# First stage of a vision tower kernel: the attention products issued ahead of the rank matmuls in every group

## The reference

```
tokens = einsum('bpi,hi->bph', patches, W) + b        # 64 patches of 28x28x3 per image, 128 features
h = concat([cls, tokens]) * pos_embed
n = layernorm(h)                                      # attention over a strictly causal window
scores = <n_t, n_s>; alpha = softmax(scores); c_t = sum alpha n_s
h = h + sigmoid(concat([c_t, n_t]) @ W_c)
z = layernorm(layernorm(h)); gate = softmax((z @ router_w + router_b) / 0.7)
mix = the two best of 16 experts: silu(z @ ew1 + eb1) @ ew2 + eb2, weighted by gate
moe = mix + 0.25 * shared expert
out = h + layernorm(h) + moe + silu(layernorm(moe) @ ff_w1 + ff_b1) @ ff_w2 + ff_b2
```

## Time and profile before

| what | value |
|---|---|
| median of three runs | 907.61 us (907.56 to 908.23) |
| span of the profiled execution | 972.0 us |
| TensorE busy in the span | 896.2 us, 92% |
| VectorE, ScalarE, GpSimd busy | 676.2, 599.5, 438.8 us |
| mean granted TensorE clock | 0.975 of full |
| DMA | 192 GB/s over the span |

### The profile page before, as it was taken

The page is one execution under the profiler, slowest core; times in us unless marked ns, Lnnn a source line. Parts: engine busy times, 40 slices in busy tenths (PEclk is TensorE's granted clock), DMA queues, the critical chain, the costliest instruction groups (busy, mean ns, idle before and its releaser), DMA issues. The chain is left out here.

```text
span 972.0 us, 22164 instructions
## 1 busy us (share of the span) xinstructions
PE 896.2 (92%) x5920; PEld 801.2 (82%) x5920; DVE 676.2 (70%) x2244; ACT 599.5 (62%) x1064; POOL 438.8 (45%) x374
## 2 busy tenths in 40 slices
PE   2999999989999999999889999999999899789999
PEld 2788888778878888888779889898999899679888
DVE  8377877757877887787556666666676675488884
ACT  3567666656666666777645565555555565477766
POOL 6012554425555545554451445455555464334342
PEclk9999999979999999999879999999999999989999
DMA  9999999977788888767137687777778675334432
GB/s 225 224 221 225 242 247 240 237 205 210 213 228 218 214 216 219 194 216 213 50 105 215 196 227 218 214 219 228 216 224 236 184 221 166 107 82 115 107 103 57
DMA packets 194299, 186.96 MB, mean 192 GB/s; under 512 B 16797, under 2 KB 168698, under 8 KB 194010
## 3 DMA queue, kind: packets, MB, share of 16 engines
q1 hardware_dynamic: 183168, 166.24, 65.2%
q0 software_dynamic: 9376, 19.42, 6.1%
q10 hardware_dynamic: 1722, 0.93, 0.5%
HBM read 150.48 MB, written 36.04 MB: 192 GB/s over the span
## 5 line engine op out<-in xcount | busy, mean ns | idle before, releaser
L1435 PE MATMUL bank<-xf,wp 128*128 128x256 f32 x1280 | 314.0, 394 | 8.4 <-ACT xf L632 5.4
L1435 PEld LDWEIGHTS bank<-xf,wp 128*128 128x128 f32 x1280 | 237.7, 192 | 51.6 <-issue 7.4
L916 POOL DMA_INDIRECT y_tok<-region,dsti x160 | 162.9, 1018 | 164.9 <-DVE region L1268 119.0
L874 POOL TENSOR_TENSOR rstd<-var,neghalf 128x4 f32<-128x4 f32 (+2 forms) x51 | 80.6, 1580 | 287.9 <-DVE var L1030 156.4
L632 ACT ACTIVATE xf<-region 128x1024 f32<-128x1024 f32 x160 | 174.0, 1137 | 18.3 <-DVE region L947 18.3
L890 POOL DMA_INDIRECT z_rows<-z,posg x130 | 157.3, 1210 | 52.5 <-issue 52.2
L798 ACT ACTIVATE region<-bank,cols 128x256 f32<-128x256 f32 x320 | 132.3, 476 | 55.2 <-PE bank L1626 37.2
L1637 PE MATMUL bank<-region 128*128 128x128 f32 x1280 | 156.8, 275 | 1.1 <-DVE region L1268 1.0
L1637 PEld LDWEIGHTS bank<-region 128*128 128x128 f32 x1280 | 150.4, 192 | 1.7 <-issue 1.5
L1626 PE MATMUL bank<-parts 128*128 128x256 f32 x960 | 136.6, 290 | 14.2 <-DVE parts L1279 8.8
L1626 PEld LDWEIGHTS bank<-parts 128*128 128x128 f32 x960 | 119.6, 190 | 25.7 <-issue 19.0
(11 more groups left out here) (183 smaller groups left out, 1232.3 us busy)
## 6 DMA issues: line engine op xcount, KB each, us to landing
region<-in_x SPq DMA_DIRECT2D x384, 196.0 KB
region<-in_L_ffn_ew SPq DMA_DIRECT2D x160, 256.0 KB
region<-z_rows SPq DMA_DIRECT2D x80, 130.0 KB
region<-y_tok SPq DMA_DIRECT2D x16, 512.0 KB, 3.6
ht_dram<-hT SPq DMA_DIRECT2D x16, 256.0 KB
r_dram<-rr SPq DMA_DIRECT2D x16, 256.0 KB
region<-ht_dram SPq DMA_DIRECT2D x16, 256.0 KB, 5.5
region<-r_dram SPq DMA_DIRECT2D x16, 256.0 KB
```

What stands on the lines that cost most here:

```text
L874: pool.tensor_tensor(dst, var, neghalf[:, 0:var.shape[1]], ALU.pow).then_inc(ready, 1)
L916: pool.indirect_dma_start(y_tok, bass.IndirectOffsetOnAxis(dsti[n % 2][:, i:i + 1], 0), yout[n % 2][:, i], None).then_inc(y_free[n % 2], 16)
L1435: ins = pe.matmul(out_cols, wp[:, s], cols_in, start=s == 0, stop=s == MAIN - 1)
```

## The change

In TensorE's `body`, `attend(g)` is called directly behind `project(g)` in all groups, and `ranks(g, nt)` behind it. Before, it stood so in the last group only, and behind `ranks` in groups 0 to 14. No instruction is added or taken away, and no semaphore is changed.

```
                 patches(10, 12)
                 project(g)
+                attend(g)
                 if fill:
-                    attend(g)
                     sh_up(5)
                 ranks(g, nt)
-                if not fill:
-                    attend(g)
```

## The result

The changed kernel took 913.26 us (median of six runs, 910.37 to 915.05), the kernel before 907.62 us in as many (907.11 to 910.35). The ratio is 1.0059, with a 95% interval of 1.0042 to 1.0076: 5.4 us slower, between 3.8 and 6.9. On a second chip session the ratio was 1.0040 (1.0022 to 1.0058), 3.6 us. The forecast of 908.9 us and its range, up to 912.0, were too low; what came is the second rival, by which positions become late in every group, and 913.26 us is a little over even its upper figure of 912.2.

A forecast was written before the change was run, and what follows sets the result against it. The prediction took VectorE's chain from m2 to xh, level with TensorE's path, as the bound. Losses of 1.1 and 0.3 us, scaled by 0.934, gave +1.3 us: 908.9 us, range 904.5 to 912.0.

The forecast's parts named there:

- the second rival: Rank waits for m2 are the profiler's; positions on VectorE late in all fifteen groups: 910.5 to 912.2 us, chance 0.15.
- The second wait of the earlier trace: TensorE's transposes of xh (L1440) wait for VectorE's xh (L1021), six times, 2.5 us; taken as showing VectorE's chain.
- the count of groups: At TensorE's ranks (L1473): eight of fifteen changed groups wait for m2, 8.1 us in all; seven have no wait.
- the sum: Four groups without wait 1.1 us, three others 0.3 us, waiting groups 0: +1.4 us, scaled by 0.934 to +1.3 us.
- Attention ahead of a rank wait: On TensorE, attend fills 5.9 us of rank waits, but the next wait for xh gives it back: 0.
- The first rival: TensorE's order decides: rank gaps are filled and xh comes in time; full effect 5.5 us, 902.1 us, chance 0.17.
- Ranks later where they did not wait: Ranks 0.89 us later make VectorE's positions and xh late: 0.21 us lost in group 7, 0.33 in group 2.
- The three groups where positions already waited: Groups 0, 5 and 14: bound 0 to 0.89 us lost each, taken as 0.1 us each, 0.3 us together.
- ScalarE: It gets th's input 0.2 to 0.9 us sooner, its patch copies likewise; worth nothing.
- The signs named beforehand: Profile after: short or no rank waits, longer xh waits, some positions waiting, m2 to xh unchanged; two outcomes would refute the forecast.

The follow-up runs named there:

- positions deferred: On VectorE, positions and what hangs on them moved behind the next group's first statistics; against the kernel before: 0.9974 with TensorE's old order, 0.9970 with the changed order.
- second and third profile: The kernel before, unedited, profiled twice more: 907.5 us (ratio 0.9996), span 904.2 us; then one run of 909.06 us, span 907.2 us.
- the eleven later profiles: Profiled executions behind the first, of the kernel before and its relatives; spans between 904.2 and 917.7 us.

## Why the prediction was wrong

*What bounds the kernel.* The chain m2, positions, h, reciprocal root, xh was read rightly, and that it is level with TensorE's path as well. The second wait of the earlier trace rows was the right one to follow. With positions deferred it disappears and the kernel becomes faster than both.

*The step that failed* is the count of groups: "Seven of the fifteen groups that the change touches (0, 1, 2, 5, 7, 13, 14) have no wait there." From it the sum priced four groups in full, three at 0.1 us and eight at nothing. In an ordinary execution all fifteen have no wait, as the second and third profile of the same kernel show. The eight rank waits, 8.1 us in all, were of one execution whose span was 64 us over the median of the runs. The prediction named that difference as what speaks for the second rival and still gave it 0.15, since "eight of fifteen groups show waits": it took the count from the very profile that the difference put in doubt. Scaling the sum by 0.934 treated the excess as if it were spread evenly. It was not. Against the second profile, L1511 of group 15 comes 25.7 us later (474.43 against 448.75), and what is behind it takes 42.1 us more. Of the 25.7 us, 10.4 lie in one step, from group 4 to group 5: 35.98 us for 25.55. VectorE and TensorE stand idle there:

```profile
203.98 1.09 DVE L947 COPY region<-region 32x1792 f32<-32x1792 f32 x1 [7.59 <-ACT hT L652]
```

```profile
200.17 3.78 PE L1435 MATMUL bank<-xf,wp 128*128 128x256 f32 x8 [3.08 <-issue]
```

Behind TensorE's 3.08 us of idle time the granted clock is 0.50 from 200 to 208 us, the lower of its two levels (1.2 for 2.4 GHz), and eight of these matmuls take 3.78 us, which take 1.97 us at 184.82. Another 11.0 us lie in the other steps from group 3 to group 13, most of them behind the late logits, and 4.3 us in the step from group 14 to group 15. Behind the first stage it was other waits, such as TensorE's for parts, here from 500 to 850 us (0.4 us, once, in the second profile):

```profile
PE bank L1626 <- DVE parts L1279: 8.8, 27, 0.7
```

*Attention ahead of a rank wait.* That the 5.9 us would be given back at xh could not be tested, as no execution since had such waits in groups 1 to 13. It was argued, and stays so. The first rival has no support: its gap is in none of the eleven later profiles in groups 1 to 13, so the rule of the Trainium skill that spoke for it (Perfetto Trace Analysis, Optimization Strategy: find the gaps on the most contended engine and make what blocks it start sooner) had nothing to work on at this place. Applied to the gap that is there in the changed kernel, xh, it holds: the deferral makes what blocks TensorE start sooner, and the ratio falls from 1.0040 to 0.9970.

*Ranks later where they did not wait.* The mechanism was right, and so was the size in an odd group. Positions moved by 0.33 us (1.36 to 1.69 behind m2, above) where 0.32 and 0.33 were worked out. Lost were 25.60 - 25.35 = 0.25 us behind an odd group (0.21 expected, and the xh transposes are 310.39 - 302.30 = 8.09 us behind L1511 where they were 256.49 - 248.61 = 7.88) and 25.99 - 25.55 = 0.44 behind an even one (0.33 expected). The 0.33 is the one term too small, by its starting point. The prediction had positions 1.79 or 1.80 us behind L1511 in both kinds of group, from groups 2 and 7. In the steady even groups of a plain execution they start at 1.70 us (275.67 - 273.97), since m2 is 0.09 us sooner there; after the change they start at 2.12 us in both kinds (278.43 - 276.31). So an even group's positions are 0.42 us later and an odd group's 0.33, with nothing and about 0.1 us in hand. Fifteen groups at 0.21 to 0.33 gave the second rival 2.9 to 4.6 us after scaling; 4.06 us are in the profiles from group 0 to 14, 3.6 and 5.4 us in the two ratios, so that the larger one lies over the rival's 4.6.

*The three groups where positions already waited.* They were given 0.1 us each. Between groups 14 and 15 the kernel before takes 448.75 - 426.49 = 22.26 us and the changed one 452.93 - 430.73 = 22.20: nothing is lost there, though positions of group 14 now wait 1.57 us in place of 0.68:

```profile
432.85 0.35 DVE L1183 TENSOR_TENSOR pp<-bank,base 128x64 f32<-128x64 f32 x2 [1.57 <-PE bank L1481]
```

The low end was right. Group 0 loses 0.03 us (25.28 for 25.25). Group 5 was not of this kind at all in a plain execution.

*ScalarE.* An earlier th was called worth nothing. With positions deferred, where its benefit would not be covered by a loss, the two orders of TensorE have 0.9974 and 0.9970: no gain that the times can tell. The profiles have 0.04 us a group, 0.6 us from group 0 to 14; which part of the new order gives it was not tested.

*The signs named beforehand.* Positions waiting in nearly all groups, stage longer by 3 us or more: that was written as what would mean the second rival, and it is what came. The xh waits of 1 to 1.4 us behind a late m2 did not come (the longest is 0.7 us), and the distance from m2 to the end of xh did not stay at 7.2 to 7.6 us: behind group 8 it is 284.64 - 276.74 = 7.90.

## What to carry to other kernels

When the span of a profile is 7% over the timed runs, its stalls are suspects: take a second profile, or price the change for an execution without them and give that case the larger chance. Where two consumers hang on one engine's order, ask for each how long after its input is ready it would really be taken up; an operand may come late at no cost up to that moment, and whatever it is later than that is paid in every iteration (0.45 us free, 0.67 and 0.89 not). And where an engine waits for a round trip to another, bookkeeping that nobody needs at once belongs into that wait, not ahead of it.

## What the runs showed of the hardware beyond the expected

One profiled execution of a program had a span of 972.0 us, where two others of the same program had 904.2 and 907.2. Among its waits of VectorE from 60 to 480 us are these for the logits' start, the lower one without a releaser in the profile:

```profile
DVE lg L1156 <- PE bank L1467: 10.9, 10, 2.3
DVE lg L1156 <- remote: 9.5, 4, 2.6
```

What caused them stays open. The granted clock, 0.975 against 0.994, accounts for a part of the longer span at most: 2.5% of 972.0 us are 24 us, and 0.6% of 904.2 are 5, so 19 of the 67.8 us between the two, by this estimate. And VectorE's branch at the loop's end costs 0.31 us before h, as in the row above at 280.04 (behind groups 4, 6, 8 and 10, and 0.38 us behind group 2; behind odd groups no such idle time stands); with positions deferred it no longer shows in the period of the groups, 25.35 us in both kinds.
